# A graph kernel in which the first norm scatters one row per node, keeps the edge tiles' rows by place, and unrolls its last stage

## The reference, cut to what matters

```python
x = layernorm(x + gcn(x, W[3], b, gamma, beta, edges))      # first norm: the rows "x2"
x = layernorm(x + message(x, src, dst, attr, weight, net))  # second norm: the result
```

## Time and profile before

| | us |
|---|---|
| median of 3 runs (1737.77 to 1739.99) | 1739.05 |
| the profiled execution | 1743.42 |
| its span, first to last instruction | 1741.7 |
| PE, DVE, ACT, POOL busy | 1375.5, 1205.7, 948.3, 975.6 |
| `order_edges` | 0 to 176.4 |
| `graph_layers` | 176.4 to 1142 |
| `finish_gcn` | 1142 to 1397.6 |
| `messages` | 1397.6 to 1642 |
| `touched` | 1642 to 1741.7 |

### The profile page before, as it was taken

The page is one execution under the profiler, slowest core; times in us unless marked ns, Lnnn a source line. Parts: engine busy times, 40 slices in busy tenths (PEclk is TensorE's granted clock), DMA queues, the critical chain, the costliest instruction groups (busy, mean ns, idle before and its releaser), DMA issues. The chain is left out here.

```text
span 1741.7 us, 27484 instructions
## 1 busy us (share of the span) xinstructions
PE 1375.5 (79%) x8020; PEld 1179.2 (68%) x8020; DVE 1205.7 (69%) x3400; ACT 948.3 (54%) x1906; POOL 975.6 (56%) x986
## 2 busy tenths in 40 slices
PE   4676699999989799999979999935454179999633
PEld 3555488888877688888768888824444068888622
DVE  7247466566665676768667778848777379999765
ACT  3462244334425677767466666428777534444576
POOL 5770667777773687877443333206777644344146
PEclk8589699999999999999989999957566589999955
DMA  2000887878777577777555566279998433323112
GB/s 61 1 2 3 259 301 263 270 256 272 247 239 275 184 253 247 255 255 247 201 185 191 199 210 213 103 227 379 412 398 358 184 92 88 94 84 92 35 75 110
DMA packets 130924, 340.37 MB, mean 195 GB/s; under 512 B 34972, under 2 KB 67220, under 8 KB 127990
## 3 DMA queue, kind: packets, MB, share of 16 engines
q1 hardware_dynamic: 74486, 175.45, 28.6%
q0 software_dynamic: 56320, 163.51, 27.9%
HBM read 166.40 MB, written 177.40 MB: 197 GB/s over the span
## 5 line engine op out<-in xcount | busy, mean ns | idle before, releaser
L1020 PE MATMUL ps_b<-yhi,whi 128*128 128x492 f32 (+1 forms) x960 | 397.1, 414 | 18.9 <-ACT aggT L912 14.3
L1020 PE MATMUL ps_b<-ylo,whi 128*128 128x492 f32 (+1 forms) x960 | 378.2, 394 | 0.0
L1020 PE MATMUL ps_b<-yhi,wlo 128*128 128x492 f32 (+1 forms) x960 | 377.8, 394 | 0.0
L912 ACT COPY aggT<-ps_b 128x492 f32<-128x492 f32 (+1 forms) x240 | 137.6, 574 | 319.8 <-PE ps_b L1020 319.7
L830 DVE BATCH_NORM_STATS2 stat<-aggT 128x6 f32<-128x492 f32 (+1 forms) x240 | 161.9, 676 | 145.6 <-ACT aggT L912 145.4
L672 POOL DMA_INDIRECT rows<-rows_out,node_at x160 | 180.8, 1130 | 110.4 <-ACT rows_out L918 63.3
L1020 PEld LDWEIGHTS ps_b<-yhi,whi 128*128 128x128 f32 x960 | 185.6, 193 | 50.2 <-ACT aggT L912 14.7
L1020 PEld LDWEIGHTS ps_b<-yhi,wlo 128*128 128x128 f32 x960 | 184.0, 192 | 38.1
L1020 PEld LDWEIGHTS ps_b<-ylo,whi 128*128 128x128 f32 x960 | 185.2, 193 | 30.2 <-issue 0.5
L679 POOL TENSOR_TENSOR X<-X,own_row 128x1016 f32<-128x1016 f32 x40 | 96.4, 2412 | 131.5 <-ACT X L896 131.3
L1253 PE MATMUL fin_ps_x<-ident,fin_X 128*123 128x128 f32 (+1 forms) x320 | 69.8, 386 | 102.8 <-DVE fin_xr L1178 73.9
(11 more groups left out here) (345 smaller groups left out, 3223.5 us busy)
## 6 DMA issues: line engine op xcount, KB each, us to landing
z<-aggT SPq DMA_DIRECT2D x30, 1016.0 KB, 5.1
z<-aggT SPq DMA_DIRECT2D x30, 984.0 KB, 6.1
x_rows<-R SPq DMA_DIRECT2D x80, 256.0 KB, 3.6
fin_xr<-x_rows SPq DMA_DIRECT2D x20, 1024.0 KB, 8.1
X<-z SPq DMA_DIRECT2D x20, 1016.0 KB, 8.1
X<-z SPq DMA_DIRECT2D x20, 984.0 KB, 7.6
fin_X<-z SPq DMA_DIRECT2D x10, 1016.0 KB, 12.6
fin_X<-z SPq DMA_DIRECT2D x10, 984.0 KB, 13.2
```

What stands on the lines that cost most here:

```text
L912: nc.scalar.copy(f.aggT[t % 2][:, j, 0:cols(t)], f.ps_b[j % 2][:, 0:cols(t)]).then_inc(x["copied"], 1)
L1020: o = nc.tensor.matmul(f.ps_b[j % 2][:, 0:n], w[:, c, j * P:(j + 1) * P], y[g % 2][:, c, 0:n], start=(c == 0 and i == 0), stop=(c == C - 1 ...
```

## The change

**The mark.** `order_edges` now also finds for each node whether it is the src of some edge (`s.flag`) and writes it as a second word beside the node's number (`s.nodeid`, `a.others`, `k.node_at` are two words wide). The same table gives each edge the place of its dst in the edge tiles: `s.base[0]` grows to 3*NC = 240 columns and `looks(0, t)` has a third multiply-and-sum. The place goes into the payload where dst was.

**The first norm.** POOL scatters only one row per node, into the result: x2 for a marked node (its final row comes from `touched`), x2 times `rstd2` for the others. For plain tiles ACT writes that row at once, since DVE multiplies `rstd` and `nmr` by the mixed factor beforehand. For edge tiles ACT writes x2 (`f.x2`, now 2 buffers of 4 tiles), DVE multiplies four tiles by the factor, and SP's queue stores the x2 rows of the block in place order (`keep`), with no index. `messages` gathers G from that table and `own` from the result.

**Smaller moves.** `l_nexti` is loaded in `messages`; eight of the weights are loaded after block 4's loads and the coefficients computed in turn 4. `touched` is unrolled: PE reads `l.sT` itself, the root, reciprocal and shift are taken for four tiles at once.

```diff
@@ order_edges
                 nc.vector.scalar_tensor_tensor(s.junk[i][t % 2][:], s.ps_look[i][:, NC:2 * NC], 1.0, s.hot_col[i][:, t, :],
                                                ALU.mult, ALU.mult, accum_out=s.dinv[i][:, t:t + 1])
+                if i == 0:
+                    nc.vector.scalar_tensor_tensor(s.junk4[t % 2][:], s.ps_look[i][:, 2 * NC:3 * NC], 1.0, s.hot_col[i][:, t, :],
+                                                   ALU.mult, ALU.mult, accum_out=s.tail[:, t:t + 1])
...
+            v.link(nc.vector.tensor_scalar(s.leaves[:], s.tail[:], SRC, None, ALU.is_ge))
+            v.link(nc.vector.scalar_tensor_tensor(s.tail[:], s.leaves[:], -SRC, s.tail[:], ALU.mult, ALU.add))
+            v.link(nc.vector.scalar_tensor_tensor(s.keyf[1][:], s.leaves[:], MARK, s.keyf[1][:], ALU.mult, ALU.add))
+            dve.wait_ge(packed, 5)
+            nc.vector.tensor_scalar(k.payload[:, :, 1], s.tail[:], float(ET * m.EPT - 1), None, ALU.min)
...
-                nc.tensor.matmul(s.ps_look[i][:, 0:2 * NC], s.hot_loT[i][:, t * P:(t + 1) * P], s.base[i][t % 2][:],
+                wide = s.base[i][0].shape[1]
+                nc.tensor.matmul(s.ps_look[i][:, 0:wide], s.hot_loT[i][:, t * P:(t + 1) * P], s.base[i][t % 2][:],
@@ finish_gcn, sync
+            def keep(b):
+                q = m.nth(b) % 2
+                sp.wait_ge(x["normed"], 4 * (b + 1))
+                rows = bass.AP(x2_dram.tensor, x2_dram.offset + 4 * m.nth(b) * m.EPT * D, [[D, m.EPT], [m.EPT * D, 4], [1, D]])
+                sp.dma_start(rows, f.x2[q][0:m.EPT, :, :]).then_inc(kept[q], 16)
+
             for b in range(3, NB):
                 sp.wait_ge(x["turned"], 4 * (b - 2))
                 sp.dma_start(f.X[b % 3][:, :, 0:cols(b)], z_in[b, :, :, 0:cols(b)]).then_inc(z_got[b % 3], 16)
                 ge(sp, x["normed"], 4 * (b - 3))
                 sp.dma_start(f.xr[b % 4][:], x_rows[b]).then_inc(x_in[b % 4], 16)
+                if m.edges(b - 4):
+                    keep(b - 4)
+                if b == 4:
+                    prep.load_late(sp)
+            for b in range(NB - 4, NB):
+                if m.edges(b):
+                    keep(b)
+            for q in range(2):
+                sp.wait_ge(kept[q], 16 * (m.NE // 2))
@@ finish_gcn, gpsimd
-                        pool.wait_ge(x["normed"], n + 1)
-                        pool.indirect_dma_start(x2_dram, bass.IndirectOffsetOnAxis(ap=k.node_at[:, i:i + 1], axis=0), f.x2[n % 8][:], None,
...
-                        pool.wait_ge(x["edge_out" if j < 2 else "plain_out"], 2 * t + j % 2 + 1)
+                        if m.edges(t):
+                            pool.wait_ge(x["made"], 4 * m.nth(t) + j + 1)
+                        else:
+                            pool.wait_ge(x["normed"], n + 1)
@@ finish_gcn, vector
-                    nc.vector.reciprocal(f.rstd2[q][:], f.std2[q][:]).then_inc(x["ready"], 1)
-                if runs(t):
-                    for j in range(2):
+                    v.link(nc.vector.reciprocal(f.rstd2[q][:], f.std2[q][:]))
+                    v.link(nc.vector.tensor_tensor(f.rstd2[q][:], f.rstd2[q][:], f.stays[:, at], ALU.mult))
+                    nc.vector.tensor_tensor(f.rstd2[q][:], f.rstd2[q][:], f.leaves[:, at], ALU.add).then_inc(x["ready"], 1)
+                    if m.plain(b):
+                        dve.wait_ge(x["ready"], b + m.nth(b) + 1)
+                        v.link(nc.vector.tensor_tensor(f.nmr[q][:], f.nmr[q][:], f.rstd2[q][:], ALU.mult))
+                        nc.vector.tensor_tensor(f.rstd[q][:], f.rstd[q][:], f.rstd2[q][:], ALU.mult).then_inc(x["ready"], 1)
+                if m.edges(t):
+                    for j in range(4):
@@ finish_gcn, scalar
+                    if m.edges(t):
+                        ge(act, kept[e % 2], 16 * (e // 2))
+                        ge(act, x["made"], 4 * (e - 1))
...
-                        nc.scalar.activation(f.out[n % 8][:], f.x2[n % 8][:], ACT.Copy,
-                                             scale=f.rstd2[q][:, j:j + 1]).then_inc(x["plain_out"], 1)
@@ EdgePrep.load
-            sp.dma_start(l.nexti[:], self.sorted[1:m.EPAD + 1, :].rearrange("(t p) w -> p t w", p=P)[:, :, 0]).then_inc(s["nexts"], 16)
@@ touched, gpsimd
+            for b in range(ET):
+                ge(pool, s["done"], b + 1)
+                pool.indirect_dma_start(out_dram, bass.IndirectOffsetOnAxis(ap=l.row[:, b:b + 1], axis=0), l.Y[b % RING], None,
+                                        bounds_check=m.N - 1, oob_is_err=False).then_inc(put[b % RING], 16)
```

More of the change, by code:

```diff
@@ L17 @@
 TINY = 1e-25
+SRC, MARK = 8192.0, 16384.0
 class Steps:
@@ L1292, in load, with load_late, weighs @@
                 sp.dma_start(dst, src).then_inc(s["loaded"], 16)
+    def load_late(self, sp):
+        with self.m.nc.allow_non_contiguous_dma(reason="small weights"):
+            for dst, src in self.late:
+                sp.dma_start(dst, src).then_inc(self.s["came"], 16)
     def starts(self, t):
-        return isinstance(t.group, int) and t.s == 0
+        return t.s == 0
+    def weighs(self, t):
+        return t.s == 4
     def unit(self, t):
@@ L1453, in messages, with _ @@
     with nc.Block() as block:
+        @block.sync
+        def _(sp):
+            with nc.allow_non_contiguous_dma(reason="one word of each sorted row"):
+                sp.dma_start(l.nexti[:], by_src[1:m.EPAD + 1, :].rearrange("(t p) w -> p t w", p=P)[:, :, 0]).then_inc(s["nexts"], 16)
+            sp.wait_ge(s["nexts"], 16)
         @block.gpsimd
@@ L1616, in touched @@
 def touched(m, k, l, out_dram):
-    nc, ET = m.nc, m.ET
+    nc, ET, D = m.nc, m.ET, m.D
     mag = l.rows[:, 0:m.EPAD]
-    names = ("mag", "exp", "log", "pos", "plus", "vec", "hcopy", "prod", "ysum", "stats", "aggr", "root", "rec", "nmr", "done", "idx2")
+    names = ("mag", "exp", "log", "pos", "plus", "vec", "prod", "ysum", "stats", "aggr", "root", "rec", "nmr", "done")
     s = {n: m.sem(f"tch_{n}") for n in names}
-    RING = 8
+    RING, GS, parts = 8, 4, 4
+    NG, per = ET // GS, ET // parts
     put = [m.sem(f"tch_put{r}") for r in range(RING)]
-    parts = 4
     part = [slice(i * m.EPAD // parts, (i + 1) * m.EPAD // parts) for i in range(parts)]
-    def x_row(b):
-        return l.X[:, bass.ds(b, 1), :].rearrange("p a f -> p (a f)")
-    def run(engine, body, first=-3, last=ET):
-        turns(engine, body, first, last, 8, ET // 8 - 2, ET, 8)
+    group = [slice(g * GS, (g + 1) * GS) for g in range(NG)]
     with nc.Block() as block:
@@ L1684, in _ @@
         def _(pe):
-            def body(t):
-                if t.runs(3):
-                    b, q = t.block(3), t.slot(3, 2)
-                    pe.wait_ge(s["hcopy"], b + 1)
-                    ge(pe, s["ysum"], b - 1)
-                    nc.tensor.matmul(l.ps[q][:, 0:P], l.hb[q][:], l.W2s[:], start=True, stop=True).then_inc(s["prod"], 1)
-            run(pe, body)
+            for b in range(ET):
+                pe.wait_ge(s["plus"], b // per + 1)
+                ge(pe, s["ysum"], b - 3)
+                nc.tensor.matmul(l.ps[b % 4][:, 0:P], l.sT[:, P * b:P * (b + 1)], l.W2s[:], start=True, stop=True).then_inc(s["prod"], 1)
         @block.vector
@@ L1703, in _, with plus @@
             dve.wait_ge(s["pos"], parts)
-            for i in range(parts):
+            def plus(i):
                 dve.wait_ge(s["log"], i + 1)
```

232 lines of the change are left out of this document (116 added, 116 removed).

## The result

The changed kernel takes 2091.57 us (median of 4 runs, 2087.34 to 2095.24); the kernel before takes 1739.52 beside it. The ratio is 1.2015, with a 95% interval from 1.198 to 1.205: 352 us slower, where 325 were forecast and 1980 to 2160 us was the range. The time is in the stage and behind the transfer that the prediction named. The profiled executions differ by 350.6 us in their spans (1741.7 and 2092.3).

A forecast was written before the change was run, and what follows sets the result against it. POOL's scatter pitch was taken to bound finish_gcn, PE messages. Terms order_edges +12, graph_layers 0, finish_gcn +325, messages +1 and touched -13 gave +325 on 1739: 2064 us, range 1980 to 2160.

The forecast's parts named there:

- The bound and the place: finish_gcn: POOL's scatters stop being the bound; SP's queue with the new stores becomes it, +325 us.
- a store of 127 partitions stays on one engine: finish_gcn's new stores: by the largest divisor up to 16, 127 partitions use one DMA engine; chance 0.83.
- The store, 40.3 forecast: finish_gcn: each block's store of 1.040 MB takes 40.3 us at 25.8 GB/s.
- 121 + 7.5: End of finish_gcn: blocks 16, 18 and 19 stored in 121 us, with 5 for scatters and 2.5 for loads.
- The circle, 57.6 forecast: finish_gcn: store delays fin_X, hence relu, norm and next store; 57.6 us for two turns, where 20.5 before.
- Seven circles: finish_gcn: seven such two-turn waits from 1190.4 take 403 us, to 1594.
- The start, -10.5 forecast: Start of finish_gcn: without the l_nexti wait and the coefficients, the first turn begins about 10.5 us earlier.
- `order_edges`, +12 forecast: order_edges: wider look, third pick and four small operations behind the loop add 12 us, bounds +4 and +16.
- The step of 0.33 us: order_edges loop: look +0.17 and third pick 0.16 us a step, at most 13 us over 40 steps.
- `touched`, -13 forecast: touched: POOL's pitch of 1.28 us a tile sets the unrolled stage; -13 us, range -9 to -15.
- The first rival: finish_gcn: store spreads over all 16 engines, two turns take 18.3 us, total 1707 (1690 to 1725); chance 0.12.
- The four-engine rival: finish_gcn: store uses four engines by its middle dimension, 10.1 us; two turns 27.4, total 1770; chance 0.05.

The follow-up runs named there:

- second group: Runs on one chip, kernel before 1742.07 us; against it cut store 1752.57, cut store with next load issued ahead 1706.80, new touched alone 1730.47.
- third group: Kernel before 1926 us; against it next load ahead alone 1.0016, with cut store 0.9551, wider look alone 1.0023; changed kernel with next load ahead 2184.50 us.
- first group: Kernel before 1939 us; changed kernel with its store cut at 112 partitions 1891.79, at 124 1959.71, on ACT's queue 2202.58, on POOL's queue 2298.36.

## Why the prediction was right, step by step

**The bound and the place.** The step on which all hung, that a store of 127 partitions stays on one engine, held: share 0.07, 26 GB/s, and a cut of the same bytes into 112 and 15 partitions takes 340 us of the stage away. It was read from loads of other partition counts; the cut at 124 moves alone at a share of 0.25, 4 engines. One reading in it was looser than it looks: the load of 125 partitions has a share of 0.46, which by itself is 7.4 engines, and I took its rate. The window holds 278 packets of under 512 bytes beside the load's 40; those 40 alone have a share of 0.31, 5 engines.

**The store, 40.3 forecast.** Right: where a store moves alone it goes at 26 GB/s (1344 to 1366, 1690 to 1740), which is 40 us for 1.040 MB. The last three in a row take from 1622.09 to 1757.3, 135 us, where the forecast set 121 + 7.5. The stores themselves are 120 of that; what was sized too low is what shares the engine with them. POOL still issues 16 scatters in this time, four blocks' worth, and by the forecast's own share (5.0 for eight) they cost 10 and not 5. This is +6 of the miss.

**The circle, 57.6 forecast, 59.5 measured.** Right in length and in what ends the wait: the last sixteenth of `fin_X` lies behind the store on its engine, and the relu starts 0.4 us behind it. One thing was not foreseen: I wrote that SP issues the transfers one behind the other, but SP's queue itself stands, 42 us in the issue of the next transfer, so that the other fifteen sixteenths come late too. They are in by 1374 and the relu does not start until 1378.83, so by the packets this standing is not what set the length; no run took it away by itself. My terms between the store's issue and the relu (2.5 + 40.3 + 2.5 + 5.0 + 1 = 51.3) measured 52.9, and the store with the scatters' shares in it took 45.0 of the 45.3 forecast for them (its packets run from 1330.9 to 1375.9). Seven circles took 416 us (block 2's norm ends at 1206.0, block 16's at 1622.1), not 403: +13.

**The start, -10.5 forecast.** Block 2's norm ends 54.4 us behind the stage's first load, where it was 58.5: -4.1, a miss of 6. Two things were wrong in it. The name in the earlier trace rows had misled me: with `l_nexti` gone, the row that follows `l_edges` in its place has the same length. And the late weights were not covered: they stand ahead of `fin_X` of block 5, for which the relu ahead of block 2's norm waits 6.77 us. SP's and ACT's rows of the changed kernel:

```profile
1155.29 0.54 SPq L1332 DMA_DIRECT2D l_edges<-by_src  x1
1155.88 15.80 SPq L1335 DMA_DIRECT2D l_bf<-in_L_gnn_bf  x1
...
1173.24 0.53 SPq L1148 DMA_DIRECT2D fin_X<-z  x1
...
1184.72 0.46 SPq L1340 DMA_DIRECT2D l_Ws<-in_L_gnn_W_in2f_s  x1
...
1189.45 0.53 SPq L1148 DMA_DIRECT2D fin_X<-z  x1
```

```profile
1200.13 2.86 ACT L1262 ACTIVATE fin_X<-fin_X,bn_shift,bn_scale 128x492 f32<-128x492 f32 x4 [6.77 <-DMA fin_X<-z]
```

The queue stood for `l_edges` and the loads ahead of it, not for `l_nexti`; which of them, was not tried. DVE was freed of the coefficients, but the first turn's norm stands behind the relu of block 3, and that waits for its load: SP issues it 21.7 us behind the stage's first load, where it was 28.8, 7.2 earlier and not 10.5. The eight late weights then take 4.7 us of SP's queue (1184.72 to 1189.45) ahead of block 5's load, and 4.1 are left. The three misses, 6 + 13 + 6, are the 25 us by which the stage's forecast was short.

**`order_edges`, +12 forecast, +8.7 measured.** The step of 0.33 us was right where nothing covers it (0.30), but it is covered in two of four steps, where I had counted it as nearly uncovered: 5.7 us for the loop. The other 3 should lie outside the loop; no run took those operations singly.

**`touched`, -13 forecast, -11.6 by itself.** Its pitch is POOL's 1.28, as forecast.

**How much of the hit is luck.** The stage's three misses have one sign, so the 27 us between 2064 and 2091.57 are not small because errors cancelled there. Outside it `order_edges` came out 3.3 us below its forecast and the last two stages 2.8 above theirs, which did cancel.

**The first rival**, that the store spreads, was wrong on this kernel but could be timed by cutting the store. It was worked out at 1707 with circles of 18.3; they are 24.2 to 25.5, and the kernel is 0.7% slower than before, not 2% faster. The step that failed in it: I gave `fin_X` 12 us to land from the end of the store's first issue, and behind 2 MB of other transfers it needs 17 from its own issue (relu at 1271.97, its load issued at 1254.62) and 18 from the store's. The order that takes it out of that place brings 17.5 to 20.1 and a total of 1707; that this is the rival's own figure is a coincidence, since the rival had no such order. The four-engine rival was likewise too quick (27.4; 35 measured).

## What to carry to other kernels

Before a plain transfer is added, look at its partition count: with 127 a megabyte stayed on one engine for 40 us, 45 with the scatters beside it, and the queue stood for 42; as 112 + 15 the queue stood for 1. The cut at 112, a multiple of 16, served better than the one at 124. Moving the store to another queue did not help: ACT then stood for 43 us in the issue, and on POOL's queue, whose issue takes 4.8, the scatters stood behind the store. A long issue row in a queue tells of what was issued ahead of it, not of the transfer that it names.

A saving of scatters (160 to 80) gained nothing on the second group's chip, 0.7% slower, until the next bound, the place of one load behind two others in SP's queue, was removed as well: then 2% faster. The order of the loads alone, tried on the third group's chip, gave nothing. In the two groups where the kernel before is slower the same edits gave more, 2.7% for the cut store alone in the first and 4.5% with the new order in the third; only in the third is it traced where this lies, in `finish_gcn` of the kernel before.

## What the runs showed of the hardware that was not expected

An issue can hold its engine for 42 us, and it is the issue of whatever stands behind the store in the same queue: in SP's queue the next load (42.06 us), and of its last three stores the first is not held and the other two are (85.16 for all three); in ACT's queue the next store (0.47 us for the first, 33.49 for the second, then 31 to 44).

While POOL issues such a store, for 4.8 us, one instruction of DVE stands with it. Of the four multiplications of 128x512 at 1467.20 three take 0.49 us and the last, which starts 0.8 us behind POOL's issue, 4.15; it ends 0.2 us behind the issue. In eight of the ten blocks one of the four takes 4.15 to 4.28. With the store on ACT's queue none of the 40 takes over 0.58 us. The last one by itself:

```profile
1469.10 4.15 DVE L1233 TENSOR_SCALAR fin_out<-fin_x,fin_rstd 128x512 f32<-128x512 f32 x1
```

The chips of the first and third group differ from the second's in three places. Two of them show in every kernel. In `order_edges` the end comes at 268 to 282 us, not at 170 to 181: from 34 to 134 us, while POOL issues its 77 scatters of single words, PE is busy for 10 us there and for 64 on the other chip (the first group's cut store, then the changed kernel):

```profile
34.00:134.00 100.00, 10.03 (x52) 6.35 (x50) 5.11 (x48) 6.02 (x21) 75.27 (x77) 0.52 0.02 1
```

```profile
34.00:134.00 100.00, 64.37 (x492) 51.74 (x490) 39.58 (x356) 55.65 (x176) 75.27 (x77) 0.76 0.02 2
```

`graph_layers`, from there to the first load of `finish_gcn`, takes 990 to 1010 us in place of 970 to 973. And on the third group's chip `finish_gcn` of the kernel before takes 309 to 311 us in place of 256, while with the new stores it is as long as on the other chip; of the first group there is no trace of the kernel before. The cause of all three stays open.
